# The recurrence of an RWKV layer in units of two value columns by two chunks, with the first states copied by Pool

## What is computed

```python
def step(s, rkvw):
    r_t, k_t, v_t, w_t = rkvw
    a = k_t[:, :, :, None] * v_t[:, :, None, :]
    out = jnp.einsum('bhk,bhkd->bhd', r_t, u * a + s)
    return (a + w_t[:, :, :, None] * s, out)
xs = tuple((jnp.moveaxis(t, 1, 0) for t in (r, k, v, w)))
_, outs = jax.lax.scan(step, s0, xs)
```

## Time and profile before

| | us |
|---|---|
| median of 3 runs | 2302.81 (2302.04 to 2303.87) |
| the profiled execution | 2301.0, its span 2299.2 |
| PE busy | 2141.9 (93%) |
| DVE busy | 1952.8 (85%) |
| ACT busy | 1260.4 (55%) |
| POOL busy | 585.2 (25%) |

### The profile page before, as it was taken

How to read it: one execution, slowest core, us unless ns; L and a number is a source line. 1 busy time by engine, 2 the same in 40 slices (tenths; PEclk the granted TensorE clock), 3 DMA queues, 4 the chain that set the end, 5 groups by cost and what they waited for, 6 DMA issues and landing times. The chain is left out here.

```text
span 2299.2 us, 41734 instructions
## 1 busy us (share of the span) xinstructions
PE 2141.9 (93%) x14176; PEld 1477.2 (64%) x14176; DVE 1952.8 (85%) x4863; ACT 1260.4 (55%) x4405; POOL 585.2 (25%) x700
## 2 busy tenths in 40 slices
PE   3698799999999999999999999999999999999866
PEld 2475576767666676767667676766767676666533
DVE  0258898989899898989989898999989899998982
ACT  1736374573838466383746648373755738374312
POOL 1131314222331422232141322224141222314200
PEclk7799899999999999999999999999999999999977
DMA  7100101001010100001010100101010010100000
GB/s 268 35 7 20 31 11 49 11 11 41 11 50 11 49 11 31 21 11 50 11 49 11 48 3 11 50 11 50 11 49 1 11 50 11 50 2 29 1 19 10
DMA packets 48978, 69.88 MB, mean 30 GB/s; under 512 B 20512, under 2 KB 26656, under 8 KB 48768
## 3 DMA queue, kind: packets, MB, share of 16 engines
q1 hardware_dynamic: 48768, 67.21, 8.9%
HBM read 50.42 MB, written 16.78 MB: 29 GB/s over the span
## 5 line engine op out<-in xcount | busy, mean ns | idle before, releaser
L1226 DVE TENSOR_TENSOR_SCAN st<-ws,st 128x256 f32<-128x256 f32 x1024 | 637.4, 686 | 0.1
L862 ACT ACTIVATE probs_or_mixes<-probs_or_mixes,least 128x128 f32<-128x128 f32 x1024 | 398.9, 403 | 117.4 <-DVE least L1173 116.3
L1215 DVE TENSOR_TENSOR st<-bank_pair,kT 128x1016 f32<-128x1016 f32 x256 | 308.0, 1203 | 88.0 <-PE bank_pair L717 88.0
L1236 DVE TENSOR_TENSOR st<-st,rT 128x1024 f32<-128x1024 f32 x256 | 317.9, 1243 | 0.0
L1173 DVE CUSTOM_DVE_ANT_0 probs_or_mixes<-bank,nmask 128x128 f32<-128x128 f32 x1024 | 231.1, 285 | 100.5 <-PE bank L566 76.0
L1108 POOL TENSOR_SCALAR rstd<-rstd 128x1 f32<-128x1 f32 x96 | 26.5, 276 | 1098.4 <-ACT cin L895 600.1
L1102 POOL TENSOR_TENSOR probs_or_mixes<-probs_or_mixes 128x512 f32<-128x512 f32 x160 | 190.1, 1218 | 341.4 <-DVE probs_or_mixes L1267 341.4
L862 ACT ACTIVATION_READ_ACCUMULATOR probs_or_mixes<-probs_or_mixes,least 128x1 f32 x1024 | 206.4, 202 | 0.0
L717 PE MATMUL bank_pair<-v_hi,sel 32*128 32x256 f32 x1024 | 193.8, 339 | 10.9 <-DVE st L1215 10.6
L717 PE MATMUL bank_pair<-v_lo,sel 32*128 32x256 f32 x1024 | 166.6, 286 | 0.0
L717 PEld LDWEIGHTS bank_pair<-v_hi,sel 32*128 32x128 f32 x1024 | 114.5, 185 | 72.3 <-issue 35.4
(11 more groups left out here) (150 smaller groups left out, 4216.3 us busy)
## 6 DMA issues: line engine op xcount, KB each, us to landing
inputs_turned<-in_ctx_turned SPq DMA_DIRECT2D x16, 512.0 KB, 3.6
inputs_turned<-in_x_turned SPq DMA_DIRECT2D x16, 512.0 KB, 4.6
xin<-in_x SPq DMA_DIRECT2D x16, 512.0 KB, 3.7
x<-xin SPq DMA_DIRECT2D x16, 512.0 KB, 4.1
keep<-x SPq DMA_DIRECT2D x16, 512.0 KB, 3.6
out<-keep SPq DMA_DIRECT2D x32, 256.0 KB, 2.0
...
```

The costliest lines, as they stand in the source:

```text
L862: last = fn(pr[:, n % 4, j, :], pr[:, n % 4, j, :], ACT.Exp, bias=least[:, n, j:j + 1], scale=-1.0, accum_out=rsum[:, n, j:j + 1])
L1215: tt(dst, src, over(kv, DU, 1), ALU.mult).then_inc(outer.sem, 1)
L1226: last = nc.vector.tensor_tensor_scan(v, ws[:, c].rearrange("p b t -> p (b t)"), v, 0.0, ALU.mult, ALU.add)
L1236: tt(v, v, over(rT[:, u // PER, :], DU, 1), ALU.mult).then_inc(weighed.sem, 1)
```

## The change

A unit becomes two value columns of two chunks (a pair of chunks has 8 units). The spread is four matmuls of 512 columns in place of eight of 256, the scan is two scans of 512 in place of four of 256, and `outer` and `weigh` keep their sizes. `reduce` has four matmuls of 512 columns in place of eight of 256, and all four reduces of a pair of chunks collect in bank 7. `readout`, `rk` and the sum of `v_hi` and `v_lo` work on two chunks at once, half as often and twice as wide, and the latter is a step of its own, `joined`. `bonus` goes to a bank of the ring, with two matmuls, once for a pair. `first` moves from ACT to POOL. The four order tables are written anew. At the start, the centring of the value weights uses banks 7 and 3 in turns.

```diff
-UNIT_D = [(0, 1, 8, 9), (4, 5, 12, 13), (2, 3, 10, 11), (6, 7, 14, 15)]
+HALF_T = 2 * T
+UNIT_D = [(4 * (w % 2) + w // 2, 8 + 4 * (w % 2) + w // 2) for w in range(2 * PER)]
...
 POOL_ORDER = """
-norm0.0+1 rk.2+2 affine0.0+1 norm0.1+1 affine0.1+1 norm1.0+1 norm1.1+1 mix.0+1 mix.1+1 mix.2+1 mix.3+1 rk.3+2 rk.0+1
...
+mix.1+1 first.13+2 first.14+2 mix.2+1 mix.3+1 first.15+2 negate.0 first.0+1 bias.0 rk.0+1 joined.0+1 first.1+1
...
-                wait(sp, first.sem, first.after(g - 1, PER * (c + 1)))
+                wait(sp, first.sem, first.after(g - 1, 2 * PER * (c // 2 + 1)))
...
                 for e in range(NC):
-                    if e == 3:
-                        pe.wait_ge(centred_v, 1)
+                    if e >= 2:
+                        pe.wait_ge(centred_v, e - 1)
...
                 wait(pe, outer.sem, outer.after(g, u))
-                for k in range(2):
-                    for part in (v_hi, v_lo):
-                        for s in range(2):
-                            d = UNIT_D[u % PER][2 * s + k]
-                            r = slice(32 * (d // 4), 32 * (d // 4) + 32)
-                            last = mm(pair[:, s, k * T:(k + 1) * T], sel[r, d % 4, :], part[r, c, :],
-                                      start=part is v_hi, stop=part is v_lo)
+                p, w = u // (2 * PER), u % (2 * PER)
+                for part in (v_hi, v_lo):
+                    for half in range(2):
+                        d = UNIT_D[w][half]
+                        r = slice(32 * (d // 4), 32 * (d // 4) + 32)
+                        last = mm(pair[:, half, :], sel[r, d % 4, :],
+                                  part[r, 2 * p:2 * p + 2, :].rearrange("p c n -> p (c n)"),
+                                  start=part is v_hi, stop=part is v_lo)
...
-                m, c = q % 2, q // 2
+                p, m = q // PER, q % PER
                 if m == 0:
-                    bonus(g, c)
+                    wait(pe, read_out.sem, read_out.after(g, p))
+                if m == PER - 1:
+                    bonus(g, p)
...
-            def first_state(g, u):
-                c, d = u // PER, UNIT_D[u % PER][0]
...
-                fn(dst, src, ACT.Copy).then_inc(first.sem, 1)
...
+            def first_state(g, u):
+                p, d = u // (2 * PER), UNIT_D[u % (2 * PER)][0]
...
+                if u % (2 * PER) == 0:
+                    pool.wait_ge(centred.sem, centred.after(g, 2 * p + 2))
+                wait(pool, summed.sem, summed.after(g, (u - SLOTS) // 2 + 1))
+                stand(pool, "pool")
+                dst = st[:, u % SLOTS, :].rearrange("p (s c b t) -> p s c b t", s=2, c=2, b=NB)[:, :, :, :, 0]
+                src = s0[:, 2 * p:2 * p + 2].rearrange("p c b (s d) -> p s c b d", s=2)[:, :, :, :, d]
+                nc.gpsimd.tensor_copy(dst, src).then_inc(first.sem, 1)
...
-                for s in range(DU):
-                    v = st[:, u % SLOTS, s * T:(s + 1) * T]
-                    last = nc.vector.tensor_tensor_scan(v, ws[:, c].rearrange("p b t -> p (b t)"), v, 0.0,
+                for half in range(2):
+                    v = st[:, u % SLOTS, half * HALF_T:(half + 1) * HALF_T]
+                    last = nc.vector.tensor_tensor_scan(v, ws[:, 2 * p:2 * p + 2].rearrange("p c b t -> p (c b t)"), v, 0.0,
                                                         ALU.mult, ALU.add)
```

More of the change, by code:

```diff
@@ L127 @@
-values.1 turn_p.8 score.12 turn_p.9 turn_p.10 reduce.2+1 turn_p.11 score.14 spread.8+1 project.0 turn_m.1+2 values.2
-turn_p.12 turn_p.13 spread.9+1 turn_p.14 reduce.3+1 flip.1 turn_p.15 spread.10+1 share.1 values.3 project.1 ffn_k.0+2
-ffn_r.0+2 ffn_k.1+2 spread.11+1 ffn_r.1+2 turn_n.0 turn_n.1 ffn_v.0+2 ffn_v.1+2 low.0
+low_rank.0+1 spread.13+2 key.0 tdecay.0+1 reduce.5+2 low_rank.2+1 spread.14+2 proj_r.0+1 spread.15+2 decay.0+1
+proj_v.0+1 proj_k.0+1 decay.1+1 spread.0+1 reduce.6+2 reduce.7+2 query.0 var.0+2 value.0 proj_r.1+1 score.0
```

173 lines of the change are left out of this document (82 added, 91 removed).

## The result

The changed kernel takes 2334.31 us (median of 4 runs, 2330.86 to 2339.55); the kernel before took 2302.43 beside it. The ratio is 1.0138, with a 95% interval of 1.0125 to 1.0150. I had predicted 2284 and a range of 2262 to 2313: wrong in sign, and outside the range.

A forecast was written before the change was run, and what follows sets the result against it. PE was taken to bound the period: -0.4 - 0.5 - 0.2 = -1.1 us, times 15 is -16.5; with drain -3 and start +1, 2301.0 became 2282.5, plus 1.8 for the median 2284 us, range 2262 to 2313.

The forecast's parts named there:

- The work hides easily; its place in the queue is what may cost.: POOL taking the copies: 3 to 11 us a period on an engine busy 36 of 132.
- PE's waits: -0.2: PE's waits in a period: lighter DVE and ACT shorten them by 0.2 us, bounds -1.2 and +1.5.
- POOL's queue making `scan` wait for `first`: On POOL and DVE: a named sign that the forecast would be wrong; no size given.
- The slower rival: SP's start state for chunk 2 lands late, ACT delays PE at decay.1: 18 us more, 2319; chance 0.2.
- The time of the rival above it, 2267: Lighter DVE and ACT queues remove nearly all 1.81 us of PE's waits: 32 us, 2267; chance 0.17.
- "-0.4" for the spread: PE's spreads: fewer, wider matmuls save 0.025 us a unit over 16 units, 0.4 us a period, bounds 0 and 0.5.
- "-0.5" for the crossings: PE's switches between whole-array and tiled steps: 46 become 40 at 0.09 us each, saving 0.5 us a period.
- Reduce 0: PE's reduces: the same columns are streamed before and after, so no time is saved.
- ahead of `project.1` 0.6 filled: PE's 0.88 us wait for DVE's gather: spread.10 fills 0.6 us of it, eaten by new waits elsewhere.
- DVE "118.7": DVE's busy time in a period: falls from 121.7 to about 118.7 us through wider scans and readout.
- The drain "-3": The end of the run, where a group's recurrence runs alone: lighter DVE saves 3 us, once.
- The start's +1: The start: centring in two alternating banks makes PE wait for evacuations, costing 1 us once.

The follow-up runs named there:

- e1: The changed kernel with joined.0 moved behind first.5 in POOL's table, in place of right behind rk.0: 2307.0 us, ratio 1.0015.
- e17: e12 with bias.0 moved one step later in POOL's table, behind rk.0: 2300.0 us, ratio 0.9986.
- e7: e1 with SP's load of state 2 moved behind the loads of the mask, x and turned x: 2304.0 us, ratio 1.0007.
- e5: e1 with each spread written as eight matmuls of 256 columns in place of four of 512: 2306.4 us, ratio 1.0019.
- e2: The changed kernel with the sixteen copies of the first states moved back from POOL to ACT: 2356.7 us, ratio 1.0229.
- e6: e1 with every scan of 512 columns written as two of 256: 2321.7 us, ratio 1.0086.
- e8: e7 with both bias steps ahead of first.0 on POOL and weigh.12 ahead of scan.13 on DVE: 2324.8 us, ratio 1.0104.
- e10: e9 with two moves in DVE's table, out.0 ahead of weigh.2 and inverse.1 ahead of readout.0: 2320.3 us, ratio 1.0072.
- e12: e9 with reduce.6 moved ahead of decay.1 in PE's table: 2317.4 us, ratio 1.0061.
- e16: e9 with bias.0 and bias.1 moved behind norm2.1 in POOL's table: 2331.0 us, ratio 1.0134.
- e3: The kernel before with only the copies of the first states moved to POOL: 2320.8 us, ratio 1.0074.
- e4: The kernel before with one added wait: mix.4 on POOL starts only after the root chain's first small instruction on DVE: 2313.6 us, ratio 1.0045.
- e9: e7 with joined.1 and first.14 moved behind mix.3 and bias.1 behind joined.0 in POOL's table: 2301.5 us, ratio 0.9992.
- e11: e2 with joined.0 moved behind norm2.0 in POOL's table: 2332.9 us, ratio 1.0124.

## Why the prediction was wrong, step by step

**The step that failed** is the one on POOL: "The work hides easily; its place in the queue is what may cost." I named the danger and then priced only the 16 copies, at 0.2 to 0.7 us each, against DVE's idle 10.85 us. The copies do take 0.36 in the mean. What I didn't look at is which of POOL's long steps the new table sets beside which DVE steps. POOL was busy beside scans for about 110 us of the span before, and for about 320 us after; what the scans took over their undisturbed time rose from 18 us (637.4 less 256 times 2.42) to 73 (669.1 less 256 times 2.33). The earlier trace rows had shown such a hold-up, 3.39 us for 2.42. Most of that DVE's idle time does take: in e1 the same sum is 84 and in e17, which is level with the kernel before, 63. What it can't take is a hold-up of the root chain, since DVE is full from the mixes to the end of the chain, and PE waits for that end.
The Trainium skill's rule that I quoted (SBUF — State Buffer, "SBUF: two separate sides") goes both ways: whichever of the two starts first has the ports for its whole instruction. The trace agrees with it: of the hit instructions L1226, L1237 and L1300 have two SBUF inputs, and those with a bank as an input (L1215, L1269) were not stretched (L1215 takes 1.21 us beside POOL and alone). L1295 and L1297 have one SBUF input and were hit too; the same section of the Trainium skill counts two-port modes in as well, and no run here shows in which mode they ran. I applied the rule to POOL's copies behind a scan, and not to DVE's root chain behind POOL's 1.27 us steps.

**"PE's waits: -0.2", bounds -1.2 and +1.5.** Measured +1.9 in a period, of which the wait at `rstd` is 1.6 (27.5 less the 3.9 of the start, over 15). The bound of +1.5 came from my rivals, which were other mechanisms. A sign of being wrong that I had named did come, POOL's queue making `scan` wait for `first`: 21.0 us in all, 1.4 a period. But it is 1.4 in e1 and e7 as well, so it is not the loss.

**The slower rival** had the sign and not the cause. SP's loads are late, as it said: POOL waits for the mask 4.4 us per period. But ACT waited for no state, and PE's wait at `decay.1` is 0.4 us and for DVE's `v_lo`; with SP's order mended (e7) the period is 0.2 us shorter than in e1, and the ratio goes from 1.0015 to 1.0007, within the intervals. (The time of the rival above it, 2267, leaves out the 1.8 us of the median; with them it is 2269.)

**"-0.4" for the spread.** Mis-sized: e5 against e1 puts it at 0 to 0.1 (in the mean of the 13 periods PE is busy 130.85 us and 130.76). A spread between whole-array steps takes 0.65 to 0.66 us instead of 0.67. In the trace spreads and scores start among one another, so attributing PE's time to one of them alone misleads: with each matmul given the time to the next one's start, the spreads seem to save 1.4 us a period, and the scores, shares and `bonus` seem to cost 1.6 more; together they take 21.7 us before and 21.8 after.

**"-0.5" for the crossings.** PE is busy 130.76 us in a period before, 130.81 after, 130.70 in e1 and 130.73 in e17: spread and crossings together brought 0.1 us at most, where the prediction gave -0.9. The count of 46 and 40 is right, so the price of 0.09 for each didn't carry over; why is open. This is a second failed step: with the root chain clear and no wait of PE over 0.4 us in its periods, e17 is 0.14% faster and not 0.8%.

**Reduce 0, ahead of `project.1` 0.6 filled.** The second is right: that wait is 4.2 us in all where it was 14.1. For the first, by the same way of counting as for the spreads, the reduces take 7.8 us a period before and 8.0 after.

**DVE "118.7".** 126.0. Undisturbed, a unit's scans take 2.33 us instead of 2.42, so 0.09 and not 0.15 per unit, 1.4 a period. The scans' hold-ups rise by 3.4 a period (73 less 18, over 16) and the root chain by 2.5 (L1295 and L1297 from 0.23 to 1.06 and 1.05, L1300 by 13.5 us over 16), and the readout falls by 0.6, as I had it: together +3.9 (-1.4 + 3.4 + 2.5 - 0.6), and 4.3 to 4.4 is what the windows show.

**The drain "-3".** Not there: from the last `key` to the end it is 323.2 us before and in e1. I had no row for a chain of scans in it, only for its busy sum. The start's +1 can't be seen.

**The clock** stood in no step. In the changed kernel's periods it falls eight times, for 8.6 us, each time behind PE's wait of 1.6 us at `rstd`. In e2, e6, e8, e10 and e12 to e16 it falls too, each time behind PE's longest wait or the one at `rstd`; in the periods of the kernel before, e1, e3, e4, e5, e7, e9, e11 and e17 it does not. The length of the wait alone doesn't tell: e11 waits 1.7 us at `turn_n` in each period and has no fall, e8 1.6 us and has one, e6 1.1 us and has five. What else it takes is open.
